# Causal attention: the output projection in three passes on split operands

## The reference, cut to what matters

```python
B, S, D = 2, 1024, 256; H, KV, HD = 16, 4, 128
q = rope(x @ wq); k = rope(x @ wk); v = x @ wv      # 16 query heads, 4 key/value heads
scores = q @ k.T / sqrt(HD), causal mask, softmax -> probs
out = (probs @ v).reshape(b, s, H * HD)
return out @ wo                                      # wo is 2048 x 256
```

## Time and profile before

| | us |
|---|---|
| median of 3 runs | 2584.09 (2581.69 to 2587.95) |
| the profiled execution, own time | 2584.05 |
| its span, first to last instruction | 2582.2 |
| causal attention, about | 1367 to 2280 in the span |

### The profile page before, as it was taken

One profiled execution on the slowest core, in us unless ns is written; L12 is line 12 of the kernel. 1 busy time (PEld: TensorE's weight loads), 2 busy tenths in 40 slices (PEclk: granted clock), 3 DMA queues, 4 the chain that ended last, 5 costly groups with the idle time before them and its releaser, 6 DMA issues. The chain is left out here.

```text
span 2582.2 us, 34414 instructions
## 1 busy us (share of the span) xinstructions
PE 2355.5 (91%) x12718; PEld 1789.1 (69%) x12718; DVE 1420.6 (55%) x2476; ACT 1121.2 (43%) x1909; POOL 1139.1 (44%) x661
## 2 busy tenths in 40 slices
PE   6959999986999977999998989999999999949997
PEld 2329999973777756898896667777777777625554
DVE  6568888865222224545665865456456555463332
ACT  3467777722121113434443554646455454521221
POOL 0438999911332322343454445444544535223443
PEclk8979999997999997999999999999999999979999
DMA  6273181228312212000001000000000001055223
GB/s 242 98 294 84 58 326 58 95 72 274 96 30 34 33 36 79 1 1 1 1 1 54 21 1 21 21 1 21 1 21 5 18 9 33 1 160 154 46 42 64
DMA packets 109335, 168.33 MB, mean 65 GB/s; under 512 B 30547, under 2 KB 78675, under 8 KB 107093
## 3 DMA queue, kind: packets, MB, share of 16 engines
q1 hardware_dynamic: 94196, 145.35, 16.1%
q0 software_dynamic: 14976, 20.78, 4.9%
HBM read 115.94 MB, written 52.32 MB: 65 GB/s over the span
## 5 line engine op out<-in xcount | busy, mean ns | idle before, releaser
L638 POOL TENSOR_TENSOR mb_dbx<-mb_ud,mb_bb 128x1024 f32<-128x1024 f32 x128 | 302.0, 2363 | 58.7 <-DVE mb_h L496 42.4
L496 DVE TENSOR_TENSOR_SCAN mb_h<-ps,mb_dbx 128x1024 f32<-128x1024 f32 x128 | 292.2, 2288 | 49.8 <-ACT ps L608 38.8
L2115 POOL TENSOR_TENSOR a_e<-a_e,a_rc 128x1024 f32<-128x1024 f32 (+5 forms) x144 | 189.0, 1321 | 267.3 <-DVE a_rc L2031 266.9
L2282 PE MATMUL ps<-a_eT,a_v 128*128 128x512 f32 x576 | 296.4, 596 | 5.1 <-ACT a_eT L2159 5.1
L2041 DVE TENSOR_REDUCE a_mx<-ps 128x1 f32<-128x1024 f32 (+7 forms) x256 | 192.6, 752 | 176.9 <-PE ps L2261 176.0
L946 POOL DMA_INDIRECT e_acc<-e_hid,e_ids x78 | 123.7, 1585 | 370.9 <-DVE e_hid L1240 356.6
L2159 ACT ACTIVATE a_eT<-ps 128x512 f32<-128x512 f32 x288 | 171.2, 594 | 241.2 <-PE ps L2272 240.6
L740 PE MATMUL ps<-mb_dg,mb_hts 128*128 128x128 f32 x2048 | 251.5, 276 | 0.4
L740 PEld LDWEIGHTS ps<-mb_dg,mb_hts 128*128 128x128 f32 x2048 | 240.4, 193 | 1.9 <-issue 1.9
L1226 DVE COPY e_work<-ps 128x256 f32<-128x256 f32 x78 | 33.1, 425 | 356.4 <-PE ps L1064 356.4
L1792 POOL TENSOR_TENSOR a_elo<-a_e,a_ehi 128x1024 fp32r<-128x1024 f32 x48 | 117.8, 2453 | 227.0 <-ACT a_ehi L1649 113.8
(11 more groups left out here) (377 smaller groups left out, 5398.4 us busy)
## 6 DMA issues: line engine op xcount, KB each, us to landing
mb_bb<-mb_db_rows SPq DMA_DIRECT2D x16, 1024.0 KB, 12.4
mb_ddiag<-mb_dg SPq DMA_DIRECT2D x1, 8192.0 KB, 22.3
mb_dg<-mb_ddiag SPq DMA_DIRECT2D x8, 1024.0 KB, 12.9
e_wg<-in_g SPq DMA_DIRECT2D x8, 688.0 KB, 10.7
e_wu<-in_u SPq DMA_DIRECT2D x8, 688.0 KB, 11.4
e_wd<-in_d SPq DMA_DIRECT2D x8, 640.0 KB, 10.8
mb_dxa<-mb_bb SPq DMA_DIRECT2D x8, 512.0 KB, 2.6
mb_dz<-mb_xz SPq DMA_DIRECT2D x8, 512.0 KB, 2.9
```

Of the source, the lines that this page charges most:

```text
L496: dve.tensor_tensor_scan(h[:, at % 2, :], pair(at % 2), dbx[:, at % 2, :], 0.0, ALU.mult, ALU.add).then_inc(s_h, 1)
L638: pool.tensor_tensor(dbx[:, at % 2, :], ud[:, kk % 2, 0, :], bb[:, n, :], ALU.mult).then_inc(s_dbx, 1)
L2115: pool.tensor_tensor(probs(i, h), probs(i, h), rc[:, q:q + 1].to_broadcast([P, (i + 1) * P]), ALU.mult).then_inc(s["en"], 1)
L2282: mm = pe.matmul(ps[:, 6 + rows[u, i] % 2, :], v[:, j, :], eT[:, k % ER, :], start=(j == 0), stop=(j == i))
```

## The change

`ao` and `wo` are each kept as a high half (rounded to fp32r) and a low half (the rest), and `out` becomes 12 fp32r matmuls in place of 4 fp32 ones: high x high, high x low, low x high for each head. ACT writes the high half of `ao` where it wrote `ao`. DVE makes the low half (`sum_low`): a 128x512 subtraction of PSUM minus high half. Its place in DVE's list is given by a counter: the entry is made at the last value of a block, the next token brings the counter to 0, and the token after that (or an `out`, if one comes first) does the subtraction ahead of its own work. PE's wait ahead of `out` and ahead of the first value two blocks on is now for this subtraction. A new token `split` stands ahead of turn (7,4) of each unit: ACT copies `wo` to its high half, POOL subtracts for the low half. `wo` itself has one buffer, reloaded once the unit's split is done. `product`, used at the end, takes the room of `cos`.

```diff
-        wo_s = sb("wo", [P, 2, REP, D])
+        wo_s = sb("wo", [P, REP, D])
+        woh = [sb("wo" + half, [P, REP, D], F32R) for half in ("hi", "lo")]
-        ao = sb("ao", [P, 2, REP, P])
-        product = sb("product", [P, 4, D])
+        ao = [sb("ao" + half, [P, 2, REP, P], F32R) for half in ("hi", "lo")]
+        product = pre.cos.rearrange("p (a d) -> p a d", a=4)
...
+                        if (i, j) == (7, 4):
+                            put("split", u, 0, 0)
...
-                if u >= 2:
-                    sp.wait_ge(s["wo"], outs[u - 2, 0] + 1)
+                if u > 0:
+                    sp.wait_ge(s["wolow"], u)
...
+            def sum_low(r):
+                dve.wait_ge(s["ao"], r + 1)
+                dve.tensor_tensor(ao[LO][:, r % 2, :, :].rearrange("p a b -> p (a b)"), ps[:, 6 + r % 2, :],
+                                  ao[HI][:, r % 2, :, :].rearrange("p a b -> p (a b)").bitcast(F32), ALU.subtract).then_inc(s["aolow"], 1)
+
             for what, u, i, h in todo:
+                for sums in list(summed_up):
+                    if sums[1] == 0 or what == "out":
+                        sum_low(summed_up.pop(0)[0])
+                    else:
+                        sums[1] -= 1
...
                 elif what == "value":
                     if late and (i, h) == (0, 0):
                         normal(*late.pop(0))
+                    if h == i:
+                        summed_up.append([rows[u, i], 1])
...
+                elif what == "split":
+                    pool.wait_ge(s["wohigh"], u + 1)
+                    pool.tensor_tensor(woh[LO][:, :, :], wo_s[:, :, :], woh[HI][:, :, :].bitcast(F32), ALU.subtract).then_inc(s["wolow"], 1)
...
+                elif what == "split":
+                    act.wait_ge(s["wo_in"], 16 * (u + 1))
+                    if u > 0:
+                        act.wait_ge(s["wo"], outs[u - 1, 0] + 1)
+                    act.activation(woh[HI][:, :, :], wo_s[:, :, :], ACT.Copy).then_inc(s["wohigh"], 1)
...
-                            pe.wait_ge(s["ao"], rows[u, i] - 1)
+                            pe.wait_ge(s["aolow"], rows[u, i] - 1)
...
-                    pe.wait_ge(s["ao"], rows[u, i] + 1)
+                    pe.wait_ge(s["aolow"], rows[u, i] + 1)
                     if i == TB - 1:
-                        pe.wait_ge(s["wo_in"], 16 * (u + 1))
+                        pe.wait_ge(s["wolow"], u + 1)
                     ring_free(token)
                     for h in range(REP):
-                        mm = pe.matmul(ps[:, bank[token], 0:D], ao[:, rows[u, i] % 2, h, :], wo_s[:, u % 2, h, :],
-                                       start=(h == 0), stop=(h == REP - 1))
+                        for x_, y_ in THREE:
+                            mm = pe.matmul(ps[:, bank[token], 0:D], ao[x_][:, rows[u, i] % 2, h, :], woh[y_][:, h, :],
+                                           start=(h == 0 and x_ == y_), stop=(h == REP - 1 and x_ == LO))
```

More of the change, by code:

```diff
@@ L1840, in attn2 @@
                  "v", "nb", "e", "rc", "en", "en_last", "xout", "xin", "spare", "wo_in",
-                 "tp", "eT", "o", "ao", "wo", "hs")
+                 "tp", "eT", "o", "ao", "aolow", "wo", "wohigh", "wolow", "hs")
         s = {n: sem(n) for n in names}
@@ L1956, in _ @@
                         sp.dma_start(dst, src).then_inc(s["w"], 16)
-                if u >= 2:
-                    sp.wait_ge(s["wo"], outs[u - 2, 0] + 1)
+                if u > 0:
+                    sp.wait_ge(s["wolow"], u)
                 kv = u % KV
-                sp.dma_start(wo_s[:, u % 2, :, :], wo[kv * REP * P:(kv + 1) * REP * P, :].rearrange("(h p) d -> p h d", p=P)).then_inc(s["wo_in"], 16)
+                sp.dma_start(wo_s[:, :, :], wo[kv * REP * P:(kv + 1) * REP * P, :].rearrange("(h p) d -> p h d", p=P)).then_inc(s["wo_in"], 16)
                 if u == 0:
@@ L2034, in normal @@
                     dve.tensor_scalar(probs(i, h), probs(i, h), rc[:, q:q + 1], None, ALU.mult).then_inc(s["en_last"], 1)
-            for what, u, i, h in todo:
+            summed_up = []
+            def sum_low(r):
+                dve.wait_ge(s["ao"], r + 1)
+                dve.tensor_tensor(ao[LO][:, r % 2, :, :].rearrange("p a b -> p (a b)"), ps[:, 6 + r % 2, :],
+                                  ao[HI][:, r % 2, :, :].rearrange("p a b -> p (a b)").bitcast(F32), ALU.subtract).then_inc(s["aolow"], 1)
+            for what, u, i, h in todo:
+                for sums in list(summed_up):
[3 more added lines that the diff above has]
+                        sums[1] -= 1
                 if what == "score":
@@ L2180, in _ @@
                         act.wait_ge(s["wo"], rows[u, i] - 1)
-                    act.activation(ao[:, rows[u, i] % 2, :, :].rearrange("p a b -> p (a b)"), ps[:, 6 + rows[u, i] % 2, :], ACT.Copy).then_inc(s["ao"], 1)
+                    act.activation(ao[HI][:, rows[u, i] % 2, :, :].rearrange("p a b -> p (a b)"), ps[:, 6 + rows[u, i] % 2, :], ACT.Copy).then_inc(s["ao"], 1)
                 if what == "project":
```

## The result

The changed kernel takes 2698.04 us (median of 4 runs, 2697.59 to 2707.28) against 2582.89 for the kernel before: ratio 1.0442, 95% interval 1.0424 to 1.0461. That is 115 us slower; the forecast was 94 us (2678, range 2645 to 2702). Its profiled span is 2695.9 us, 113.7 above that of before.

What follows compares the result with a forecast made beforehand. PE was taken to bound the kernel, busy 91% of the span. Profiled 2584.05 us + 65.8 (waits net of the matmuls' gain) + 28.4 (clock) gave 2678.2, say 2678; range 2645 to 2702.

Steps and rivals of the forecast that it cites:

- The gain of the matmuls: Each out on PE: 12 fp32r matmuls take 1.44 us against 1.73, gaining 0.29 an out, 2.32 a unit.
- sum_low at 0.69 us: DVE's 128x512 subtraction from PSUM, taken as 0.69 us between bounds of 0.42 and 1.22.
- The waits: PE ahead of outs, units 1 to 6: out(5) 4.17 us, out(4) 4.87, out(3) 0.2, out(1) 2.36; the others no stall.
- The split of wo and the reload at nothing: ACT's copy and POOL's subtraction at turn (7,4), and SP's reload of wo: hidden, 0 us; 10 if cover failed.
- The exponential's 0.52 us: PE's wait for an exponential in each unit, put down to DVE being late: goes, 0.52 us a unit won.
- The clock: PE at half clock behind the idles at out(5), out(4), out(1): 1.5 + 1.5 + 1.0 = 4.0 us a unit, 28.4 in all.
- The bound of 3 x 2.2: Upper bound of the slow clock's cost per unit, for slow stretches with more of 1.2 GHz; lower bound 0.
- Unit 0: First unit, with chores on DVE: out(3) starts 14.6 us later; 13.7 us net without the clock, 4.4 for the clock.
- the first (waits without slow clock, 2650): Rival: the stalls ahead of the outs come but PE's clock holds; 2650 us, chance 0.10.
- The second (low half ready in time, 2565.5): Rival: DVE reaches sum_low ahead of the projection, so only the matmuls' gain counts; 2565.5 us, chance 0.04.
- The third, another phase from unit to unit: Rival: stalls at out(5) and out(4) halved as DVE and PE fall into another phase; 2632 us, chance 0.06.

Runs made afterwards that it cites:

- the run without the wait: Changed kernel without DVE's low half of ao: third pass reuses the high half, PE waits for ACT's copy; 2570.37 us, ratio 0.9943.
- the projections behind: Changed kernel with the subtraction right behind its block's last value and, in DVE's list alone, project(3) and project(4) behind value(4,4) and value(3,3); 2593.13 us.
- the fill: Changed kernel with 48, 60 and 24 small throwaway bf16 matmuls ahead of the waits of out(5), out(4), out(1) in units 0 to 6; 2663.20 us.

## Why the prediction was right

It held in its mechanism, and in size to 94 of 115 us; the clock's price was too small, and the upper bound that it had been given is what took the result into the range. Step by step:

- **The gain of the matmuls** (2.32 us a unit): 2.2 us in four of the units 1 to 6 in the run without the wait. Right.
- **sum_low at 0.69 us**: 0.68 to 0.69. Right.
- **The waits.** Counted from start to start, as the prediction did, out(5) is delayed by 4.07 us (predicted 4.17), out(4) by 4.90 (4.87), out(3) by 0.34 (0.2). Out(1) idles 2.10 us by the profile's count, which takes off the last 0.2 us of the matmul before: with that 2.3 (2.36, where the prediction's own figures give 1733.2 - 1730.87 = 2.33). Out(7), out(6), out(2), out(0) wait in no unit from 1 to 6. Right to 0.15 us each.
- **The split of wo and the reload at nothing**: no out waits for either, and the reload costs nothing. The split costs 1.5 us in all, in two units, by the detours shown in the run without the wait: 1.17 and 0.29 us in the trace of the change. The prediction looked for a wait for the split itself and not at the DVE instructions that run beside POOL's subtraction.
- **The exponential's 0.52 us, which "comes of DVE being late", would go**: wrong. It is still there in every unit. ACT's exponential waits for PE's last transpose of block 1, whose room it takes, as its row says:

```profile
1772.47 1.11 ACT L2163 ACTIVATE a_e<-ps,a_nb 128x1024 f32<-128x1024 f32 x1 [2.25 <-PE ps L2297]
```

  PE itself holds this chain, so no lateness of DVE enters. 0.5 us a unit, 3 in all.
- **The clock** (4.0 us a unit, 28.4 in all) was the term that was sized too small. One of its two bases, the wait of 2.36 us ahead of the slow window of the earlier trace rows, is this row of before:

```profile
1375.00 0.79 PE L2258 MATMUL ps<-h_qkhi,h_wmhi 128*128 128x512 f32 x1 [2.36 <-DVE a_e L2074]
```

  From the trace after, the time in which PE worked at 1.2 GHz, halved, is 5.1, 7.5, 3.3, 5.6, 5.0 and 7.5 us for units 1 to 6, mean 5.7, and 8.5 in unit 0, of which the kernel before had 1.7 as well: 41 us in all. The mean clock of the windows says the same: (1 - 0.96) x 123.7 = 5 us for unit 1. Two things were missing in my 1.5 + 1.5 + 1.0. Of the twelve waits of 3.9 and 4.7 us in units 1 to 6, five were followed by 6.8 us of the slow clock, not 3.4 (both in units 2 and 6, one in unit 4), and the shortest of the three, 2.1 us, brought it down in six of the seven units. The bound of 3 x 2.2 that I had written held on average, not in every unit.
- **Unit 0** (13.7 + 4.4 = 18.1 us): measured 23.1. Out(4) started 15.7 us later against the unit's first out (predicted 14.0), out(3) 19.1 (14.6). Of the 5.0 us that are missing, 2.4 are the clock's (6.8 in place of 4.4: 30.7 us of that unit ran at 1.2 GHz, 17 of them with PE at work). About as much is more waiting: PE idles 28.7 us there against 10.1 before, 16.3 net of the matmuls' gain, where 13.7 were forecast. Why these waits came out longer no run takes apart.

Sum for units 1 to 6: 11.6 of waits - 2.3 of matmuls + 5.7 of clock = 15.0 us a unit; measured 15.1 (751.8 - 661.0, over six). With unit 0 at 23.1 and unit 7 at - 0.3 this gives 113.6; ahead of the first out 1.8 us are less and behind the last 2.0 more, which leads to the 113.7 between the spans.

Of the rivals, the first (waits without slow clock, 2650) was refuted by the slow stretches in the trace and by the fill. The second (low half ready in time, 2565.5) was the price of another kernel, and a little too low: with other lists 2573 was reached, and without any low half 2570. The third, another phase from unit to unit, did not occur: the waits repeat to 0.02 us.

Open is why five of these twelve waits come with a slow stretch of double length; no run was made on that. Nor does the length of a short wait tell alone whether the clock falls: the wait of 1.8 us ahead of out(1) brought it down in three of the units 1 to 6 in the run with the subtraction one step earlier, and in none of them with the projections behind.

## What to carry to other kernels

When a step is given to another engine, what counts is not that engine's load but what stands ahead of the new instruction in its list at the moment it is wanted; read it off two timelines laid side by side, for every place in the loop. DVE had 45% of its time free here and still cost 115 us, and a new order of its list alone brought 105 of them back with no work removed. Price a wait on TensorE with its slow clock behind it: here 93 us of waits brought 41 us more. And look at what the added work does to instructions that run beside it, not only at what waits for it.

## What the runs showed of the hardware

The slow clock was dearer than one row of before suggested: with waits of 2 to 5 us in units 1 to 6 came stretches of 3.4 or 6.8 us at half the clock (1.2 GHz), in all but one case, and useless bf16 matmuls of 0.06 us each in these waits, which left gaps of 0.8 to 1.4 us, kept it at 1.00 in units 1 to 6. On TensorE the 12 fp32r matmuls of an out stand 0.12 us apart, 1.44 us in all, as the rows of the attention before had it, against 1.73 us for plain fp32; from the start of an out that does not wait to the next matmul it is 1.51 us, but the out also starts 0.08 us sooner behind the matmul ahead of it. And a large subtraction on POOL was not harmless to DVE: beside one of 2.35 us, two DVE instructions of 128x8 took 1.65 and 0.96 us; their median is 0.17.
